# Three of four row tiles are normed, turned, rounded and routed inside the head attention; the expert stage handles the last and finds places ahead of its splits

## What is computed

```python
qkv = x @ Wqkv.T + bqkv                              # 16 heads of 32, q k v
attn = softmax(q @ k.T / sqrt(32)); vals = attn @ v
x = x + vals @ Wo.T + bo                             # head attention
h = (x - mean) / sqrt(var + 1e-5)                    # layernorm of each row
logits = h @ router_w + router_b                     # 8 experts
gates = softmax over the two largest logits
expert(h) = (silu(h @ w1) * (h @ w3)) @ w2           # D = 512, H = 256
x = x + sum of the 2 chosen experts * gate + both shared experts
```

## Time and profile before

| | |
|---|---|
| median of three runs | 948.42 us |
| the profiled execution | 947.51 us, span 945.7 us |
| mean granted TensorE clock | 0.915 |
| TensorE busy | 787.9 us (83%) |
| VectorE busy | 599.1 us (63%) |
| ScalarE busy | 366.8 us (39%) |
| GpSimd busy | 142.5 us (15%) |
| head attention ends | 809.2 us |
| first routed block starts | 852.0 us |
| last DMA of the expert outputs starts | 925.2 us |

### The profile page before, as it was taken

The page is one execution under the profiler, slowest core; times in us unless marked ns, Lnnn a source line. Parts: engine busy times, 40 slices in busy tenths (PEclk is TensorE's granted clock), DMA queues, the critical chain, the costliest instruction groups (busy, mean ns, idle before and its releaser), DMA issues. The chain is left out here.

```text
span 945.7 us, 37813 instructions
## 1 busy us (share of the span) xinstructions
PE 787.9 (83%) x17278; PEld 656.7 (69%) x17278; DVE 599.1 (63%) x1134; ACT 366.8 (39%) x724; POOL 142.5 (15%) x390
## 2 busy tenths in 40 slices
PE   3698679998979998979998889787697967759995
PEld 1445679998979998979988889777554844424442
DVE  2777447775766875765866775547455867792225
ACT  2577415333524334424334421111266743351231
POOL 3020210411320311311211311101000000030003
PEclk9899789999989999999999999897798877688998
DMA  9957990236192354390373370604385401624524
GB/s 341 343 106 143 234 184 5 54 72 179 19 205 81 54 99 153 46 234 25 54 136 116 59 175 4 136 3 135 132 281 142 149 12 24 202 103 97 135 70 153
DMA packets 179546, 115.75 MB, mean 122 GB/s; under 512 B 145788, under 2 KB 158132, under 8 KB 176188
## 3 DMA queue, kind: packets, MB, share of 16 engines
q1 hardware_dynamic: 168944, 101.50, 42.6%
q10 hardware_dynamic: 8700, 6.56, 2.2%
q0 software_dynamic: 1744, 5.27, 1.9%
HBM read 61.94 MB, written 12.85 MB: 79 GB/s over the span
## 5 line engine op out<-in xcount | busy, mean ns | idle before, releaser
L1021 PE MATMUL banks<-qa,ctxT 128*128 128x64 f16 x3744 | 125.4, 198 | 22.3 <-issue 10.5
L1021 PEld LDWEIGHTS banks<-qa,ctxT 128*128 128x128 f16 x3744 | 121.6, 101 | 24.6 <-issue 11.5
L972 PEld LDWEIGHTS banks<-wall,whhT 128*128 128x128 f16 x3456 | 111.5, 100 | 13.4 <-issue 7.2
L972 PE MATMUL banks<-wall,whhT 128*128 128x64 f16 x3456 | 113.7, 195 | 6.5 <-issue 5.8
L972 PE MATMUL banks<-qa,wall 128*128 128x64 f16 x3456 | 105.0, 193 | 3.1 <-DVE qa L783 2.8
L972 PEld LDWEIGHTS banks<-qa,wall 128*128 128x128 f16 x3456 | 102.6, 98 | 3.4 <-DVE qa L783 3.0
L1040 PE MATMUL banks<-qa,wall 128*128 128x64 f16 (+1 forms) x1872 | 91.7, 197 | 9.4 <-issue 7.5
L1040 PEld LDWEIGHTS banks<-qa,wall 128*128 128x128 f16 (+1 forms) x1872 | 90.9, 101 | 8.5 <-issue 8.5
L1040 PE MATMUL banks<-wall 128*128 128x64 f16 (+1 forms) x936 | 90.5, 197 | 0.0
L1040 PEld LDWEIGHTS banks<-wall 128*128 128x128 f16 (+1 forms) x936 | 86.1, 101 | 1.7 <-issue 1.7
L553 ACT ACTIVATE wall<-wall 128x832 f32<-128x832 f32 x24 | 21.5, 897 | 138.5 <-DVE wall L745 138.5
(11 more groups left out here) (263 smaller groups left out, 1497.8 us busy)
## 6 DMA issues: line engine op xcount, KB each, us to landing
wall<-in_ctx_dram SPq DMA_DIRECT2D x17, 1024.0 KB, 9.5
wall<-in_L_ffn_routed_w_dram SPq DMA_DIRECT2D x23, 512.0 KB, 7.9
unit<-in_ctx_dram SPq DMA_DIRECT2D x6, 1024.0 KB, 7.8
xg_scratch<-room SPq DMA_DIRECT2D x1, 3840.0 KB, 20.4
y_scratch<-room ACTq DMA_DIRECT2D x15, 256.0 KB, 2.0
ctxT<-in_L_xattn_gru_wih_dram SPq DMA_DIRECT2D x3, 1024.0 KB, 17.6
ctxT<-in_L_xattn_gru_whh_dram SPq DMA_DIRECT2D x1, 3072.0 KB, 26.0
ctxT<-in_L_attn_Wqkv_dram SPq DMA_DIRECT2D x12, 256.0 KB, 8.2
```

The costliest lines, as they stand in the source:

```text
L972: mm = pe.matmul(dst[o], a, b, start=start, stop=True, skip_group_check=True)
L1021: mm = pe.matmul(score[n][:, t * K:(t + 1) * K], a, q, start=(k == 0), stop=(k == 3 * DC - 1), skip_group_check=True)
```

## The change

It moves the work between head attention and experts on the row tiles 0 to 2 into the head attention, and reorders the expert stage.

In the head attention: `add_y` of tiles 0 to 2 also starts the reciprocal root (`root_seed`), and is placed ahead of `values_out` and `vals_low` of its pass. GpSimd finishes the root (`rsqrt_on`, ten steps on 128x1) and norms the tile into `e.xn`. Behind `project(2)` TensorE turns tiles 0 and 1 and routes them, tile 2 behind `project(3)`; ScalarE and VectorE make the halves of each (`tile_high`, `tile_low`), straight from the turning bank. The router is now in float16 halves: its weights are split in pass k = 4 by two VectorE operations, and a tile takes eight matmuls of 16 and 8 columns. Of the four DMAs of the last row move, two go to ScalarE's queue. The router weights are loaded at the end of the sync queue's expert loads of this stage.

In the expert stage: VectorE norms tile 3 alone; TensorE starts with `up(0)`, then turns and routes tile 3, and counts behind `up(1)`. The halves of the unturned rows (`rows_high`, `rows_low`) are made tile by tile. `choose` and `find_places` come ahead of all `wall_low` chunks, and a scatter waits only for the halves of its tile. The diff, cut to its core:

```diff
+def tile_halves(e, t):
+    at = RT * D + D + D * ((t + 1) % RT)
+    return e.free[2][:, at:at + D].bitcast(F16).rearrange("p (i c r) -> p i c r", i=2, c=DC)
...
+def turn_tile(pe, c, e, bank, t):
+
+    pe.wait_ge(e.x_ready, t + 1)
+    for dc in range(DC):
+        mm = pe.transpose(bank[:, dc * P:(dc + 1) * P], e.xn[:, t, dc], c.ident32[:])
+    mm.then_inc(e.x_turned, 1)
...
+def tile_high(act, e, bank, t):
+
+    act.wait_ge(e.x_turned, t + 1)
+    act.copy(tile_halves(e, t)[:, 0], bank.rearrange("p (c r) -> p c r", c=DC)).then_inc(e.x_hi, 1)
...
+def tile_low(dve, e, bank, t):
+
+    dve.wait_ge(e.x_hi, t + 1)
+    dve.tensor_tensor(tile_halves(e, t)[:, 1], bank.rearrange("p (c r) -> p c r", c=DC), tile_halves(e, t)[:, 0],
+                      ALU.subtract).then_inc(e.x_lo, 1)
...
+def router_products(pe, e, t):
+
+    at = 2 * t * NE
+    pe.wait_ge(e.rw_lo, 1)
+    pe.wait_ge(e.x_lo, t + 1)
+    for dc in range(DC):
+        pe.matmul(e.route[:, at:at + 2 * NE], tile_halves(e, t)[:, 0, dc], e.rw16[:, dc].rearrange("p i n -> p (i n)"),
+                  start=(dc == 0), stop=True, skip_group_check=True)
+    for dc in range(DC):
+        mm = pe.matmul(e.route[:, at:at + NE], tile_halves(e, t)[:, 1, dc], e.rw16[:, dc, 0],
+                       start=False, stop=True, skip_group_check=True)
+    return mm
...
+            sp.dma_start(e_all.rw[:], dram.router_w.rearrange("(c p) n -> p c n", p=P)).then_inc(e_all.r_in, 16)
+            sp.dma_start(e_all.rb_row[:], dram.router_b.partition_broadcast(P)).then_inc(e_all.r_in, 16)
             for t in range(RT):
 
                 sp.wait_ge(vals_out, 4 * (t + 1))
-                for ii in range(4):
-                    sp.dma_start(valsT[32 * ii:32 * ii + 32, :, t * P:(t + 1) * P],
-                                 vals[:, ii:HC:4, t * P:(t + 1) * P]).then_inc(moved[t], 16)
+                for ii in range(4 if t + 1 < RT else 2):
+                    move_values(sp, t, ii)
...
+            st = Steps(pool, pool_done)
+            for t in range(RT - 1):
+                one = slice(t, t + 1)
+                pool.wait_ge(seeded, t + 1)
+                rsqrt_on(pool, st, var[:, one], rstd[:, one], tmp[:, one], more[:, one], root_out)
+                pool.wait_ge(root_out, t + 1)
+                pool.tensor_scalar(e_all.xn[:, t], rows[:, t].rearrange("p (c r) -> p c r", c=DC), e_all.mv[:, t, 0:1],
+                                   rstd[:, one], ALU.subtract, ALU.mult).then_inc(e_all.x_ready, 1)
...
+            act.wait_ge(vals_out, 4 * RT)
+            for ii in range(2, 4):
+                move_values(act, RT - 1, ii)
             wall_high(act, e_all, IN_PROJECT + B - 3, IN_PROJECT + B - 1)
+            for t in range(2):
+                tile_high(act, e_all, turn_bank(t), t)
             vals_high(RT - 1)
             wall_high(act, e_all, IN_PROJECT + B - 1, IN_HEADS)
+            tile_high(act, e_all, turn_bank(2), 2)
...
-                st(dve.bn_aggr(e_all.mv[:, t], e_all.stats[:, t]))
+                st.after(st(dve.bn_aggr(e_all.mv[:, t], e_all.stats[:, t])))
+                dve.tensor_scalar(var[:, t:t + 1], e_all.mv[:, t, 1:2], LN_EPS, None, ALU.add).then_inc(var_out, 1)
+                if t + 1 < RT:
+                    dve.wait_ge(var_out, t + 1)
+                    root_seed(dve, st, var[:, t:t + 1], rstd[:, t:t + 1], seeded)
...
+                if k == 4:
+                    dve.wait_ge(e_all.r_in, 32)
+                    dve.tensor_scalar(e_all.rw16[:, :, 0], e_all.rw[:], WS, None, ALU.mult).then_inc(e_all.rw_hi, 1)
+                    dve.wait_ge(e_all.rw_hi, 1)
+                    dve.scalar_tensor_tensor(e_all.rw16[:, :, 1], e_all.rw[:], WS, e_all.rw16[:, :, 0], ALU.mult, ALU.subtract)\
+                        .then_inc(e_all.rw_lo, 1)
+                if k >= 5 and k % 2 == 1:
+                    add_y((k - 5) // 2)
                 if k >= 1:
                     values_out(k - 1)
                 if k >= 3 and k % 2 == 1:
                     vals_low((k - 3) // 2)
-                if k >= 5 and k % 2 == 1:
-                    add_y((k - 5) // 2)
                 if k >= 3:
                     wall_low(dve, e_all, IN_PROJECT + k - 3, IN_PROJECT + k - 2)
             values_out(B - 1)
             add_y(RT - 2)
             wall_low(dve, e_all, IN_PROJECT + B - 3, IN_PROJECT + B - 1)
+            for t in range(2):
+                tile_low(dve, e_all, turn_bank(t), t)
             vals_low(RT - 1)
             wall_low(dve, e_all, IN_PROJECT + B - 1, IN_HEADS)
             add_y(RT - 1)
+            tile_low(dve, e_all, turn_bank(2), 2)
...
             project(RT - 2)
+            pe.wait_ge(shifted, B)
+            for t in range(2):
+                turn_tile(pe, c, e_all, turn_bank(t), t)
+            for t in range(2):
+                router_products(pe, e_all, t)
             project(RT - 1)
+            turn_tile(pe, c, e_all, turn_bank(2), 2)
+            router_products(pe, e_all, 2)
...
-            pool.wait_ge(x16_hi, 1)
-            pool.wait_ge(x16_lo, 1)
             pool.wait_ge(placed, 1)
             for t in range(RT):
+                pool.wait_ge(x16_lo, t + 1)
...
-            for t in range(RT):
-                act.wait_ge(x_turned, t + 1)
-                act.copy(xT[:, :, t * P:(t + 1) * P], yb[:, t, :].rearrange("p (c r) -> p c r", c=DC)).then_inc(x_out, 1)
-            act.wait_ge(x_out, RT)
-            act.copy(xs[:, 0], xT).then_inc(x_hi, 1)
-            act.wait_ge(x_ready, RT)
-            act.copy(x16[:, :, 0], xn).then_inc(x16_hi, 1)
+            def rows_high(t):
+                act.wait_ge(e.x_ready, t + 1)
+                act.copy(x16[:, t, 0].rearrange("p (c r) -> p c r", c=DC), e.xn[:, t]).then_inc(x16_hi, 1)
+
+            for t in range(LAST):
+                rows_high(t)
             for b in range(NALL + 2):
                 if b == 2:
                     act.wait_ge(gexp_in, 1)
                     act.activation(col[:, 2], col[:, 2], ACT.Exp).then_inc(gexp_out, 1)
                 if b < NALL:
                     tanh_of(b)
+                if b == 0:
+                    tile_high(act, e, yb[:, LAST], LAST)
+                    rows_high(LAST)
                 if 1 <= b <= NALL:
                     turned_high(b - 1)
...
-                st.after(st(dve.tensor_tensor(lg, route[:, 0:RT * NE].rearrange("p (t n) -> p t n", n=NE),
-                                              rb_row[:].unsqueeze(1).to_broadcast([P, RT, NE]), ALU.add)))
+                logits = route[:, 0:2 * RT * NE].rearrange("p (t i n) -> p t i n", i=2, n=NE)
+                st.after(st(dve.scalar_tensor_tensor(lg, logits[:, :, 0], 1.0 / WS, rb_row[:].unsqueeze(1).to_broadcast([P, RT, NE]),
+                                                     ALU.mult, ALU.add)))
+                st.after(st(dve.scalar_tensor_tensor(lg, logits[:, :, 1], 1.0 / WS, lg, ALU.mult, ALU.add)))
...
-            normalise(dve, st, rows, xn, e.mv, small, x_ready)
-            dve.wait_ge(x_hi, 1)
-            dve.tensor_tensor(xs[:, 1], xT, xs[:, 0], ALU.subtract).then_inc(x_lo, 1)
+            def rows_low(t):
+                dve.wait_ge(x16_hi, t + 1)
+                dve.tensor_tensor(x16[:, t, 1].rearrange("p (c r) -> p c r", c=DC), e.xn[:, t],
+                                  x16[:, t, 0].rearrange("p (c r) -> p c r", c=DC), ALU.subtract).then_inc(x16_lo, 1)
+
+            var, rstd, tmp = (e.root[:, j, LAST:] for j in range(3))
+            rsqrt(dve, st, var, rstd, tmp)
+            dve.tensor_scalar(e.xn[:, LAST], rows[:, LAST].rearrange("p (c r) -> p c r", c=DC), e.mv[:, LAST, 0:1], rstd,
+                              ALU.subtract, ALU.mult).then_inc(e.x_ready, 1)
+            gated(0)
+            tile_low(dve, e, yb[:, LAST], LAST)
+            for t in range(2):
+                rows_low(t)
             choose()
-            dve.wait_ge(x16_hi, 1)
-            dve.tensor_tensor(x16[:, :, 1], xn, x16[:, :, 0], ALU.subtract).then_inc(x16_lo, 1)
+            for t in range(2, RT):
+                rows_low(t)
+            find_places()
             for b in range(NALL + 2):
-                if b == 1:
-                    find_places()
                 if b == 4:
                     weigh()
-                if b < NALL:
+                if 1 <= b < NALL:
                     gated(b)
                 if 1 <= b <= NALL:
                     turned_low(b - 1)
...
-            for t in range(RT):
-                pe.wait_ge(x_ready, t + 1)
-                for dc in range(DC):
-                    mm = pe.transpose(yb[:, t, dc * P:(dc + 1) * P], xn[:, t, dc * P:(dc + 1) * P], c.ident32[:])
-                mm.then_inc(x_turned, 1)
-            pe.wait_ge(x_out, RT)
-            pe.wait_ge(r_in, 32)
-            for t in range(RT):
-                for dc in range(DC):
-                    mm = pe.matmul(route[:, t * NE:(t + 1) * NE], xT[:, dc, t * P:(t + 1) * P], rw[:, dc],
```

(32 more changed lines are left out.)

12 lines of the change are left out of this document (3 added, 9 removed).

## The result

The changed kernel takes 938.02 us in the median of 12 runs (932.52 to 941.87), the kernel before 947.03 us in the median of the 12 runs beside them. The ratio is 0.9901 with a 95% interval of 0.9875 to 0.9928, so 9.4 us less (6.8 to 11.8), where 3.8 us less had been forecast. A second measurement of the changed kernel gave 0.9888 (0.9837 to 0.9940).

What follows compares the result with a forecast made beforehand. The bound was the start of `up(4)`, set by the places path with VectorE's splits 2.0 us behind. Expert stage -5.3 and head attention +1.5 made -3.8 us against the profiled 947.5: 943.7 us, range 939.8 to 948.6.

Steps and rivals of the forecast that it cites:

- The chain and its two paths: Expert stage: `up(4)` waits for VectorE's last chunk at 37.5 us, the places path with row load hidden at 36.0.
- The start of `find_places`: Expert stage: `find_places` starts 15.5 us in, when the count behind `up(1)` ends; `up(4)` starts 5.3 us earlier.
- the upper clock: Rival, expert stage: TensorE at 2.4 GHz for `up(1)` gives 941.7 us, for `up(0)` as well 939.6; chance 0.25.
- The head attention: Stage before the experts: with the added tile work it ends 1.1 to 2.0 us later, taken as 1.5.
- VectorE's list behind `project(2)`: End of head attention: dense VectorE work of 14.3 us, with router matmuls and block change 15.8.
- GpSimd's lock: Tile 2's root and norm in head attention: VectorE loses 0.8 us to GpSimd, between bounds 0 and 11.8.
- the reorder of `add_y`: Passes 5 and 7: `add_y` fills VectorE's idle time; `norm` 1.4 us earlier, `project(2)` 0.9 to 1.9 earlier.
- The two queues: Last row move: two queues save two issues of 0.60 us but are worth nothing; ScalarE's 1.2 us is hidden.
- ScalarE's `tanh`: Expert stage: early `find_places` delays ScalarE's later chunks and the `tanh` of `b = 1`; costed at nothing.
- the router's weights: Pass 4: two VectorE operations, 0.4 us, lie ahead of a 5 us projection; their DMAs are issued long before.
- the slower rival: Head attention from `add_y(2)`: GpSimd and VectorE shut each other out, VectorE loses 11.8 us, 954.7 us; chance 0.08.
- The lower clock in the head attention: Rival: `project(2)` at the lower clock, VectorE's dense list starts 2.4 to 3.5 us later, 946.1 to 947.2; chance 0.17.

Runs made afterwards that it cites:

- e1: Changed kernel with `find_places` put back into pass b = 1, behind the first five chunks; ratio to the kernel before 0.9908.
- e2: Kernel before with `find_places` alone moved ahead of the b loop, so ahead of all splits; ratio 0.9996.
- e5: Changed kernel with two chunks moved ahead of `gated(0)` into VectorE's idle time; ratio to the kernel before 0.9880.
- e7: Changed kernel with all four DMAs of the last row move on SyncE's queue; ratio to the kernel before 0.9873.
- e3: Changed kernel with three chunks moved ahead of `gated(0)`, the third needing expert 5, still loading; ratio to the kernel before 0.9937.
- e9: Kernel before with one edit, `add_y` ahead of `values_out` and `vals_low` in passes 5 and 7; ratio 0.9963.
- e10: Changed kernel with root and norm of tiles 0 to 2 on VectorE instead of GpSimd; ratio to the kernel before 0.9917.
- e12: Changed kernel with idle TensorE matmuls added in four places, a repeat in more rounds; median 927.84 us, ratio to the kernel before 0.9812.
- e11: The changed kernel itself, measured once more on the same chip as the kernel with idle matmuls; median 938.56 us, ratio to the kernel before 0.9888.

## Why the prediction was wrong

Two steps failed, each by about 2.5 us. `find_places` was put at 15.5 us into the expert stage and stood at 12.7, so that stage gave 7.9 us and not 5.3. And the head attention was to end 1.5 us later and ended 1.0 earlier by the change. The mechanism, VectorE's chunks ahead of the places path, was right.

**The chain and its two paths: right.** `up(4)` is released by VectorE's last chunk, with the places path behind; e1, e2 and e5 show both. From `find_places` to the last chunk I summed 22.0 us (3.7 and 18.3), and 22.0 it is.

**The start of `find_places`: the step that failed in the expert stage.** The sum had 15.5 us; it was 12.7, and 13.5 or 13.6 where `up(0)` is wholly at the lower clock (e7, e5). Up to the end of the router it had 8.8 and 6.9 were measured. `up(0)` took 4.4 us for 5.2, turning tile 3 took 0.6 for 1.0, and the eight router matmuls, priced at 0.144 each from the float32 router, 1.15 us, all end within 0.35 in float16 (within 0.36 in e3, at the lower clock). Then came the clock for `up(1)`: the sum had 5.1 us at the lower one, and it was 2.75 in all profiles but e3's. At 5.1 it would have ended at about 12 and held up the count; at 2.75 it is off the path, and the count starts at 10.7, behind `choose`. It takes 2.0 us for 1.6.

The reading behind this choice was wrong. I had argued from rows 4 that small matmuls don't bring the clock up. In stretches of 1 us (columns as in rows 4) the kernel before shows more:

```profile
815.00:816.00 1.00, 1.00 (x6) 1.00 (x6) 0.00 (x0) 0.73 (x2) 0.00 (x0) 0.50 1.04 371
...
817.00:818.00 1.00, 0.85 (x8) 0.85 (x8) 0.00 (x0) 0.97 (x2) 0.00 (x0) 1.00 1.11 359
...
819.00:820.00 1.00, 1.00 (x10) 1.00 (x10) 0.94 (x1) 1.00 (x2) 0.00 (x0) 0.90 1.09 364
...
820.00:821.00 1.00, 1.00 (x7) 1.00 (x6) 1.00 (x1) 0.83 (x1) 0.00 (x0) 0.50 1.05 380
```

Behind the transposes of 812.80 to 816.49 the clock was at 2.4 GHz, and it fell again at about 820 us, within the float32 router matmuls, with TensorE busy all the time. In the new order `up(0)` brings it up and only 2.3 us of turning, waiting and eight short matmuls lie between its end and `up(1)`. So of the rivals the upper clock came true in its first form: places at 13.5 and 941.7 us, and most of the rest of the way to 938 is the head attention.

**The head attention: forecast 1.5 later, was 1.0 earlier, the second step that failed.** (From `norm(5)` it is 1.9, but 0.9 of that is the clock's.) Two terms were mis-sized. The larger is VectorE's list behind `project(2)`: I summed 15.8 and 0.8 for GpSimd, 16.6; 14.7 were measured (796.65 to 811.34). Of the 1.9, the router matmuls are 0.8 and GpSimd's lock 0.4; most of the rest is the tenth of a microsecond by which VectorE's operations overlap one another (two chunks take 1.2 us from start to start and not 1.4), which I had left out. The other is the reorder of `add_y`. Counted as above, `project(2)` came 2.1 us earlier for 0.9 to 1.9 forecast. For pass 5 I had 1.4 us and measured 1.5 (778.03 to 779.20 while the kernel was 2.7 us behind at the end of `project(0)`). Pass 7 adds 0.5 ahead of `project(2)`; I had named it and then folded it into 0.9 to 1.9 for both passes, taking half of pass 5's off for the clock. Behind `project(2)` the reorder brings more, as `values_out(7)` and the row move come earlier: 3.0 us in all where it stands alone (e9), about twice `add_y`'s 1.55 us, one for each pass. It pays for the tile work, 2.0 us by e9, with 1.0 left over.

**The two queues, ScalarE's `tanh`, the router's weights: right at nothing** (e7; 0.3 at `norm(5)`).

**GpSimd and VectorE: right in kind, not the slower rival.** Timeline of tile 2's root:

```profile
799.44 0.52 POOL L89 TENSOR_TENSOR e_root<-e_root 128x1 f32<-128x1 f32 x1
...
803.62 1.86 DVE L1764 SCALAR_TENSOR_TENSOR wall<-unit,wall 128x512 f16<-128x512 f32 x2
...
803.86 2.42 POOL L1453 TENSOR_SCALAR unit<-unit,e_mv,e_root 128x512 f32<-128x512 f32 x1
```

Six of GpSimd's ten steps of 0.19 last 0.52 to 0.70 beside VectorE's chunks and `vals_low`, the other four, beside `tile_low`, stay at 0.19 to 0.23; its norm takes 2.42. VectorE's two chunks there take 1.86 instead of 1.47, and that is nearly all it loses: its nine chunks take 6.54 us, and 6.16 in e10 with no GpSimd beside them.

By the rule of the Trainium skill (SBUF — State Buffer, Who interferes with whom), as the prediction worked it out, each of GpSimd's steps would hold VectorE too, for 3.1 to 4.5 us in all. The measurement decides: VectorE lost 0.4, and GpSimd, whose six steps lost 2.3 us together, waits for VectorE far more than the other way.

**The lower clock in the head attention** as the rival had it, at `project(2)`, is seen in none of the profiles with the tiles' root on GpSimd (2.75 to 2.8 us in each). The clock does scatter in passes 1 to 4 and at `project(1)` (3.3 to 4.9 us). That eight of eleven profiles of kernels built on the changed one have 3 us more ahead of `norm(5)`, and none of the three built on the one before, may be chance or a cost of the change that the forecast doesn't have; this stays open, as nothing was run for it.

## What to carry to other kernels

Sum each engine's list against the wait that ends last, and look for the second wait behind it before crediting an edit: here moving `find_places` forward was worth 0.5 us (e2, e1) and taking out the work ahead of it 7.4. An operation that stands behind a wait for another engine, moved ahead of it, was worth its whole length each time it recurs, 3.0 us for the two here (e9), as much as the tile work costs and 1.0 more. Price a new form of instruction by its own kind, not by the nearest one of another type: float32 router matmuls misled by a factor of three. And read the clock in stretches short enough to show which work it rose or fell behind.

## What was not expected of the hardware

Idle TensorE was paid for behind the idle time. In four places of the changed kernel it waited 3 to 6 us, then ran its next dense work (2.75 us at full clock) in 4.2 to 4.9 us, most of it at 1.2 GHz; 66 matmuls that compute nothing, put into the waits, kept it at 2.4 GHz there and took about 1% off the kernel (e12 against e11). GpSimd's norm of 128x512 from SBUF takes 2.1 us at the least in these profiles, and up to 2.96 beside VectorE's operations, where VectorE takes 0.55.
